# Padding the context to 128 rows and starting a routed feed-forward layer before its router is done, in a fused two-layer kernel

## The reference

```python
x = x + tanh(g_xattn[0]) * masked_cross_attention(layernorm(x), ctx, masks)   # 16 heads
x = x + tanh(g_ffn[0])   * ffn0(layernorm(x))
x = x + tanh(g_xattn[1]) * slot_attention(layernorm(x), ctx)                  # 3 rounds, GRU
x = x + tanh(g_ffn[1])   * capacity_moe(layernorm(x))                         # 32 experts, top 2
```

```python
def ffn0(xt):                       # 896 x 128; 16 experts of 64, one shared expert of 64
    scores = sigmoid(xt @ gate_w.T)
    _, idx = top_k(scores + gate_b, 4)
    w = take(scores, idx); w = w / w.sum() * 2.5
    comb = zeros(T, 16).at[tokens, idx].add(w)
    y = sum(comb[:, e, None] * (silu_and_mul(xt @ w13[e].T) @ w2[e].T) for e in range(16))
    return y + silu_and_mul(xt @ w13_s.T) @ w2_s.T        # the shared expert has no weight
```

## Time and profile before

| | us |
|---|---|
| median of 3 runs (lowest, highest) | 637.12 (636.85, 638.19) |
| the profiled execution, its own time | 635.04 |
| span of the profile, first to last instruction | 633.3 |
| item loop, first to last L1436 | about 96 to 162 |
| ffn0, from the logits to the last `down` | about 185 to 244 |

### The profile page before, as it was taken

One profiled execution on the slowest core, in us unless ns is written; L12 is line 12 of the kernel. 1 busy time (PEld: TensorE's weight loads), 2 busy tenths in 40 slices (PEclk: granted clock), 3 DMA queues, 4 the chain that ended last, 5 costly groups with the idle time before them and its releaser, 6 DMA issues.

```text
span 633.3 us, 16642 instructions
## 1 busy us (share of the span) xinstructions
PE 498.6 (79%) x5784; PEld 373.9 (59%) x5784; DVE 383.0 (60%) x1148; ACT 328.1 (52%) x953; POOL 218.6 (35%) x406
## 2 busy tenths in 40 slices
PE   3885988777777997799999999999999857019930
PEld 2622225454753443688888888788888844009920
DVE  0579855565536544478777787787778744304512
ACT  2464844444221222587878787778787813005410
POOL 8293942223210000244444444344444410440035
PEclk9996978999786999799999999999999976559975
DMA  8994743443079984200000499900000069330122
GB/s 288 250 241 124 193 138 101 116 114 108 22 169 239 208 161 167 101 2 3 3 1 0 109 238 233 195 10 2 3 0 0 2 246 432 143 104 4 38 56 69
DMA packets 46843, 73.39 MB, mean 116 GB/s; under 512 B 4613, under 2 KB 40374, under 8 KB 45638
## 3 DMA queue, kind: packets, MB, share of 16 engines
q1 hardware_dynamic: 42588, 59.93, 37.4%
q0 software_dynamic: 1472, 8.72, 3.8%
q10 hardware_dynamic: 2730, 4.03, 2.1%
HBM read 69.06 MB, written 3.60 MB: 115 GB/s over the span
## 4 chain that ended last, share of the span: by engine, by line
PE 49%; DVE 20%; ACT 11%; issue 6%; DMA 6%; POOL 6%; ACTq 1%; POOLq 0%; DVEq 0%; SPq 0%
PE ps L1537 10%; ACT work L829 6%; PE ps L1551 6%; PE ps L1474 4%; PE ps L1663 3%; PE ps L1675 2%; PE ps L1508 2%; PE ps L1582 2%; DMA early_w<-in_ctx_blk 2%; POOL xe_scratch L716 2%; DMA region<-in_ctx_blk 2%; DVE sumsq L954 2%; DVE ps L1160 2%; POOL early_w L721 2%; PE ps L1354 2%
## 5 line engine op out<-in xcount | busy, mean ns | idle before, releaser
L829 ACT ACTIVATE work<-ps,nb,rkey 125x56 f32<-125x56 f32 x576 | 176.4, 404 | 52.2 <-DVE nb L1163 45.3
L1537 PE MATMUL ps<-work,region 128*64 128x96 f32 (+1 forms) x2304 | 116.9, 252 | 7.0 <-DVE work L1223 4.8
L1537 PEld LDWEIGHTS ps<-work,region 128*64 128x64 f32 (+1 forms) x2304 | 99.6, 137 | 18.9 <-issue 5.5
L1551 PE MATMUL ps<-region,work 125*64 125x129 f32 x1152 | 72.5, 273 | 4.5 <-POOL work L687 3.1
L687 POOL TENSOR_TENSOR work<-work,rs 125x336 f32<-125x336 f32 x96 | 71.9, 749 | 7.5
L1551 PEld LDWEIGHTS ps<-region,work 125*64 125x64 f32 x1152 | 64.1, 136 | 5.3 <-POOL work L687 3.6
L685 POOL TENSOR_TENSOR rs<-rs,rkey 125x6 f32<-125x6 f32 x96 | 19.2, 200 | 124.2 <-DVE rs L1175 124.2
L1160 DVE TENSOR_REDUCE ps<-ps 125x6 f32<-125x336 f32 x96 | 49.0, 510 | 18.6 <-PE ps L1537 18.1
L1171 DVE TENSOR_REDUCE sm<-work 125x6 f32<-125x336 f32 x96 | 47.4, 494 | 1.2 <-ACT work L829 0.6
L1382 PE MATMUL ps<-xln,folded 128*128 128x448 f32 x64 | 29.8, 591 | 10.3 <-ACT region L756 10.3
L954 DVE TENSOR_REDUCE sumsq<-region 125x12 f32<-125x1536 f32 (+1 forms) x16 | 27.7, 1746 | 7.9 <-ACT region L741 7.9
(11 more groups left out here) (294 smaller groups left out, 997.9 us busy)
## 6 DMA issues: line engine op xcount, KB each, us to landing
region<-in_w SPq DMA_DIRECT2D x6, 2048.0 KB, 18.1
region<-in_ctxT SPq DMA_DIRECT2D x16, 750.0 KB
early_w<-in_ctx SPq DMA_DIRECT2D x16, 672.0 KB
region<-in_ctx SPq DMA_DIRECT2D x16, 672.0 KB
work<-in_ctxT_blk SPq DMA_DIRECT2D x22, 187.5 KB
early_w<-in_w POOLq DMA_DIRECT2D x1, 4096.0 KB, 12.4
region<-in_ctx_blk ACTq DMA_DIRECT2D x11, 187.5 KB
early_w<-in_ctx_blk ACTq DMA_DIRECT2D x10, 187.5 KB
```

Source lines behind the costliest of these rows:

```text
L829: i = act.activation(shares_of(a, h)[:, c, :], ps[:CP, 2 + 2 * a + h, c * S:(c + 1) * S], ACT.Exp, bias=nb[:, a, q:q + 1], scale=rkey[:, b ...
L1537: mm = pe.matmul(ps[r0:r1, 2 + 2 * a + h, c * S:c * S + WIDE], keysT[:, s, c0 + r0:c0 + r1], qT[:, p, a * S:a * S + WIDE], start=True, sto ...
L1551: mm = pe.matmul(ps[i * COL:(i + 1) * COL, bank, 0:KW], A[:CP, i, h, c * S:c * S + COL], keys[:, 2 * p + i, h * CH + c, :], start=(h == 0 ...
```

## The change

Two things, in one diff. First, the host pads the 125 rows of each context block and each sequence to 128 with zeros (`ctx` and `ctx_blk`), and the kernel loads 128 partitions in one transfer where it loaded 125 partitions, or 112 and 13. Computation still reads 125. Second, ffn0 runs the shared expert as steps 0 and 1, which need no router weights; it has six buffers `hh` for first halves instead of two, and does the first halves (`hidden`, silu, multiply) of steps 0 to 6 and `down` of 0 and 1 while the router runs; `hidden(7)` follows the transposition. The reciprocal `rkey` moves from the router into step 9 of the loop.

```diff
-                for p0, p1 in ((0, 112), (112, CP)):
-                    sp.dma_start(dst[p0:p1, :], ctx_b[bass.ds(b, 1), p0:p1, :].rearrange("a p c -> (a p) c")).then_inc(done, 16)
+                sp.dma_start(dst, ctx_b[bass.ds(b, 1), :, :].rearrange("a p c -> (a p) c")).then_inc(done, 16)
...
-                    for p0, p1 in ((0, 112), (112, CP)):
-                        sp.dma_start(keys[p0:p1, s, :, 0:128],
-                                     ctx_b[g * GB + s, p0:p1, :].rearrange("p (c d) -> p c d", c=CC)).then_inc(ld_keys[s], 16)
+                    sp.dma_start(keys[:, s, :, 0:128], ctx_b[g * GB + s].rearrange("p (c d) -> p c d", c=CC)).then_inc(ld_keys[s], 16)
...
-                act.dma_start(ictx[k][:KP, :, :], t["ctx_blk"][bass.ds(blk, 1), :, :].rearrange("a (p c) d -> (a p) c d", c=KC)).then_inc(ld_item[k], 16)
+                act.dma_start(ictx[k], t["ctx_blk"][bass.ds(blk, 1), :, :].rearrange("a p (c d) -> (a p) c d", c=KC)).then_inc(ld_item[k], 16)
...
+            def ffn0_up(j):
+                p = F0 if j < 2 else 128
+                v.wait_ge(e0_act, j + 1)
+                if j >= HH_BUFS:
+                    v.wait_ge(e0_y, j - HH_BUFS + 1)
+                v.tensor_tensor(hh[j % HH_BUFS][:p, :], sg[j % 2][:p, :], ps[:p, 2 * (j % 2) + 1, 0:HALF], ALU.mult).then_inc(e0_up, 1)
...
-            v.wait_ge(rk_sd, 1)
-            v.reciprocal(rkey[:, :, :], rms[:, :, :]).then_inc(rk_ok, 1)
+            for j in range(5, FIRST_UP):
+                ffn0_up(j)
             v.wait_ge(combT_mm, 1)
...
             hidden(0)
             hidden(1)
+            pe.wait_ge(ld_ffn0, 32)
+            pe.wait_ge(sc0_ok, 1)
+            for j in range(2):
+                hidden(j + 2)
+                down(j)
+            for j in range(4, FIRST_UP):
+                hidden(j)
             pe.wait_ge(comb_ok, 1)
...
+            for j in range(2, FFN0):
+                if j + 1 < FFN0:
+                    shares(j + 1)
+                if j + FIRST_UP - 1 < FFN0:
+                    hidden(j + FIRST_UP - 1)
+                down(j)
...
+        "ctx": padded(ctx.reshape(B, CP, CC * D)),
...
+        "ctx_blk": padded(ctx.reshape(B * KB, KP, KC * D)),
```

More of the change, by code:

```diff
@@ L36 @@
 PARTS = 96
+FFN0 = 2 * (PAIRS + 1)
+HH_BUFS = 6
+FIRST_UP = 7
 CP, CC = 125, 12
@@ L234, in build_program @@
         sg = [carve(HALF, "early") for _ in range(2)]
-        hh = [carve(HALF, "early") for _ in range(2)]
-        keys = region[:CP, 0:GB * CC * KW].rearrange("p (s c d) -> p s c d", s=GB, d=KW)
+        hh = [carve(HALF, "early") for _ in range(HH_BUFS)]
+        keys = region[:, 0:GB * CC * KW].rearrange("p (s c d) -> p s c d", s=GB, d=KW)
         keysT = region[:, GB * CC * KW:GB * CC * KW + GB * M].rearrange("p (s m) -> p s m", s=GB)
@@ L807, in _ @@
             act.activation(sc0[:, :, :].rearrange("p n e -> p (n e)"), ps[:, 4, 0:NT * E0], ACT.Sigmoid).then_inc(sc0_ok, 1)
-            for j in range(2 * (PAIRS + 1)):
-                p = 128 if j // 2 < PAIRS else F0
+            for j in range(FFN0):
+                p = F0 if j < 2 else 128
                 act.wait_ge(e0_mm, j + 1)
@@ L1129, in _ @@
                 v.tensor_copy(combT[:PARTS, half(h)], ps[:PARTS, 6 + h, 0:HALF]).then_inc(combT_ok, 1)
[L1131 to L1141 removed]
+            for j in range(2, FFN0):
+                ffn0_share(j)
+                if j + FIRST_UP - 2 < FFN0:
+                    ffn0_up(j + FIRST_UP - 2)
+                if j == 9:
+                    v.wait_ge(rk_sd, 1)
+                    v.reciprocal(rkey[:, :, :], rms[:, :, :]).then_inc(rk_ok, 1)
+            v.wait_ge(e0_y, FFN0)
             for h in range(2):
@@ L1466, in hidden @@
             def hidden(j):
-                pair, h = divmod(j, 2)
-                p = 128 if pair < PAIRS else F0
+                h = j % 2
+                p = F0 if j < 2 else 128
                 if j >= 2:
@@ L1477, in shares, with down @@
             def shares(j):
-                pair, h = divmod(j, 2)
-                if pair < PAIRS:
-                    if j >= 2:
-                        pe.wait_ge(e0_h, j - 1)
-                    pe.matmul(ps[:, 6 + j % 2, 0:HALF], pair_sel[:PARTS, pair, :], combT[:PARTS, half(h)],
-                              start=True, stop=True).then_inc(e0_share, 1)
-            pe.wait_ge(ld_ffn0, 32)
+                if j >= 4:
+                    pe.wait_ge(e0_h, j - 3)
+                pe.matmul(ps[:, 6 + j % 2, 0:HALF], pair_sel[:PARTS, j // 2 - 1, :], combT[:PARTS, half(j % 2)],
+                          start=True, stop=True).then_inc(e0_share, 1)
+            def down(j):
+                if j < 2:
+                    pe.wait_ge(e0_up, j + 1)
+                else:
+                    pe.wait_ge(e0_h, j - 1)
+                w, x = (w2s[:, :], hh[j][:F0, :]) if j < 2 else (w2p[:, j // 2 - 1, :], hh[j % HH_BUFS])
+                pe.matmul(ps[:, 4 + j % 2, 0:HALF], w, x, start=(j < 2), stop=(j >= FFN0 - 2),
+                          skip_group_check=True).then_inc(e0_y, 1)
             hidden(0)
             hidden(1)
+            pe.wait_ge(ld_ffn0, 32)
[5 more added lines that the diff above has]
+                hidden(j)
             pe.wait_ge(comb_ok, 1)
@@ L1497, in _ @@
             mm.then_inc(combT_mm, 1)
+            hidden(FIRST_UP)
             pe.wait_ge(combT_ok, 2)
-            shares(0)
-            def down(j):
-                pair, h = divmod(j, 2)
-                if pair < PAIRS:
-                    pe.wait_ge(e0_h, j + 1)
-                else:
-                    pe.wait_ge(e0_up, j + 1)
-                w, x = (w2p[:, pair, :], hh[j % 2]) if pair < PAIRS else (w2s[:, :], hh[j % 2][:F0, :])
-                pe.matmul(ps[:, 4 + h, 0:HALF], w, x, start=(pair == 0), stop=(pair == PAIRS),
-                          skip_group_check=True).then_inc(e0_y, 1)
-            last = 2 * (PAIRS + 1)
-            for j in range(last):
-                if j + 1 < last:
-                    if j:
-                        hidden(j + 1)
+            shares(2)
+            for j in range(2, FFN0):
+                if j + 1 < FFN0:
                     shares(j + 1)
+                if j + FIRST_UP - 1 < FFN0:
+                    hidden(j + FIRST_UP - 1)
                 down(j)
-            pe.wait_ge(e0_h, 2 * PAIRS)
+            pe.wait_ge(e0_h, FFN0 - 2)
             pe.matmul(ps[:, 6, 0:128], wq1[:, :], wk1[:, :], start=True, stop=True).then_inc(g1_mm, 1)
```

38 lines of the change are left out of this document (18 added, 20 removed).

## The result

The changed kernel takes 615.11 us, the median of four executions (613.48 to 618.59), beside 636.99 us for the kernel before on the same chip: a ratio of 0.966, interval 0.961 to 0.971. Two later measurements gave 0.965 (0.961 to 0.970) and 0.968 (0.964 to 0.973). The forecast was 620.4 with a range of 616.0 to 628.5: faster was right, and the gain of 21.9 us is 5.2 larger than the 16.7 forecast, 0.9 beyond the edge of the range. The profiled execution took 618.59, the slowest of the four; its span is 616.9.

What follows compares the result with a forecast made beforehand. The prediction took waits for block rows to bound the item loop, and the router, then PE, to bound ffn0. Gains of 9.0 and 7.7 us from 635.04 gave 618.3 profiled, median 620.4, range 616 to 628.5.

Steps and rivals of the forecast that it cites:

- Cost and gain 0: Prologue context and slot attention keys: one transfer instead of two changes nothing, the key loads being covered by ffn0.
- The block's rows: Item loop: the 128-partition transfer takes 2.75 us instead of 4.28, gaining 9.0 us.
- (2.75 + 6.1) / 3: Item loop period: one wait for rows plus work per three items, 2.95 us an item instead of 3.41.
- next in line: Item loop: work between two waits, 5.46 us for two items, 2.73 an item, still below 2.95.
- The bound of 11.2: Item loop: gain of 11.2 us if the rows' transfer takes 2.42 us, like the transposed block alone.
- Rivals B and D: B: transposed block limits item loop, gain 1.5 us, 0.12; D: transfer no shorter with more engines, 627.3 us, 0.06.
- E: Item loop: both transfers meet on all 16 engines, the transposed block lands later, kernel slower; chance 0.04.
- ffn0: Work moved from the PE-bound loop into the router: the end moves from 244.17 to 236.4, gaining 7.7 us.
- rival C: ffn0: clock stays low longer, the loop starts 1.7 to 5.1 us later, median 622 to 625.5; chance 0.13.
- Still PE: ffn0's last six steps, without `hidden`: PE needs 0.94 us a step, DVE 0.62, so PE sets the pace.
- The sum of the two terms: Whole kernel: 635.04 - 9.0 - 7.7 = 618.3 us profiled, median 620.4; both terms hold, chance 0.60.
- `rkey` at nothing: ffn0: the 1.35 us reciprocal on DVE moves into a loop step with room for it; priced at 0.

Runs made afterwards that it cites:

- no_second_keys: The kernel before without the second eight sequences' key transfers; they compute with the first eight's keys. Slot attention stage 274.0 us.
- ctx128: The kernel before with only the prologue's context and the keys loaded as one transfer of 128 partitions: 633.89 us, ratio 0.995.
- keys128: The kernel before with only the slot attention's keys as one transfer of 128 partitions, the prologue keeping its two: ratio 1.000.
- after_third: The changed kernel, unaltered, measured again beside the run of the two priced edits: 618.60 us, ratio 0.968.
- after_again: The changed kernel, unaltered, run once more for more executions and a second profile: 613.65 us, ratio 0.965.
- rows_ffn: The kernel before with block rows in 128 partitions and the new ffn0 order, context and keys loaded as before: 620.21 us, ratio 0.972.
- keys64_64: The kernel before with each sequence's keys as two transfers of 64 partitions: ratio 0.999.

## Why the prediction was right and wrong

**The step that failed** is the part on the context and the keys: "Cost and gain 0". It looked for cover at the first eight sequences alone, and there it was right: they come in 19 us faster and nobody waits for them. The transfers of the second eight run from 357 to 413 us, beside a PE that works, and in the old form the blocks of PE's instructions came late beside them. That is worth about 1.3 us in the three parts. The rest of the stage's 2.8 stands behind the last score: 25.9 to 26.7 us with the keys in one transfer, 27.5 to 27.9 with the old ones. In that stretch PE's clock was at 0.50 for 7 to 10 us in the one and for 16 to 17 in the other. `no_second_keys`, without the wait, has the long end as well (28.0, with 15 us at 0.50), so this half hangs on the clock, and what moves the clock there is not settled. In the medians the part is 3.2 us by `ctx128` and 3.1 as a difference, but nothing by `keys128`, each known to about 2.5 us: the stage shows it, the totals alone would not. The price of 0 had no bound on the side of a gain, and so the range ended at 616.0. That the time fell outside it and not inside is in part chance: it missed the edge by 0.9 us, and the median of `after_third`, 618.60, lies within.

**The block's rows** were sized at 9.0 and gave 10.3 in the stage, 9.9 by the first and last scores of the two profiles. The transfer is as forecast, 2.6 for 2.75. What was wrong is the sum (2.75 + 6.1) / 3: it kept one wait in three items, but the waits became rarer (two in the 20 items of this profile, four in that of `after_again`), and the item fell to 2.86, close to the 2.73 of the work that the prediction named as next in line. The bound of 11.2 held. Rivals B and D are out: the landing that POOL waits for is at 3.16, and the transfer did get shorter. So is E; the transposed block gained from the new shape too.

**ffn0** was sized at 7.7 and gave 6.4 between the two profiles, 6.3 in the mean: the mechanism held, the term was too large. From `hidden(0)` to the first `shares` it took 18.13 us (17.6 forecast). The first two `hidden` ran at 0.50, as the forecast had them, and took 184.79 - 179.21 = 5.58 us (6.09 forecast). The five `hidden` and two `down` behind them took 194.82 - 184.79 = 10.03 us where the sum had 9.05. That is not the clock, which was at 0.96 in the first of these windows and at 1.00 after: ahead of the loop a `hidden` took 1.71 us (184.79 to 186.50) and a `down` 0.94 (to 187.44), not the 1.51 and 0.75 of the loop, which the sum took over. So rival C is out: none of the moved records ran at the low level. The Trainium skill, page "TensorE: Matmul & The Clock Gate", section "What's actually happening", says that the low level is the default and that activity releases it. The trace agrees: the clock rose at about 184 us, after PE had worked without a pause since 179.21; but what the prediction drew from that page for this rival did not come.

From the first `shares` to the end it took 31.16 us (30.4 forecast): in the last steps `down` waits for DVE's second multiply, 1.02 at 223.50 with 0.18 of idle time ahead. "Still PE" was not quite true there.

**The sum of the two terms** was right: `rows_ffn` is the kernel that the sum describes, 620.2 measured for 620.4 forecast. That the two agree so closely is luck: one term is 1.3 short and the other 1.4 long. `rkey` at nothing was right: no step of the loop waits at it.

**Left open:** some 2 us of the whole gain that no stage shows. Two profiles of the changed kernel differ by 5.8 us in span: 2.7 of it ahead of the first scores, and 2.2 from the logits to the last `down`, which begin at 0.50 in the one and at full clock in the other.

## What to carry to other kernels

A transfer priced at nothing needs a cover for every place at which it runs, not for the first one, and for what moves beside it, here the blocks of the program's own instructions. When a wait that ended a turn gets shorter, recompute the turn from the work that is left, instead of subtracting the same saving from each wait. Asking for data sooner is no gain by itself: both trials put the asking engine's own work or wait on the path and lost 9 to 16 us.

## What the runs showed of the hardware

- Only transfers over all 128 partitions were fast: 30 ns in the mean for a packet of 512 bytes and 285 to 313 GB/s in the second group (301 in the window above), at a DMA share of 0.89 to 1.00. With 64, 112 or 120 partitions, alone or in pairs, it was 44 to 51 ns and 220 to 256 GB/s, at a share of 1.09 to 1.16. The transposed keys beside them, the same in all forms, slowed as well: 249 to 261 ns for a packet of 6000 bytes beside the fast form, 319 to 384 beside the others.
- The Trainium skill, page "DMA: Bandwidth & Descriptors", section "Rules for kernel authors", says not to split a transfer into two partition halves. `keys64_64` agrees: 55.8 us for the first eight sequences, against 37.7 in one transfer. The same page of the Trainium skill, section "The descriptor swizzle", says that in a transfer of 128 partitions each engine writes one port of SBUF. No run here shows a port, so whether this is the reason is open.
- While keys were loaded in the slow forms, PE stood still for 0.17 to 1.58 us in the middle of runs of matmuls, each time until 1.3 to 1.6 us after a 16 KB block of instructions had come in.
